# Smaller causal masks and a reordered first part, and a rearranged seam between attention and experts, in a one-core transformer block

## The reference, cut to what matters

```python
x = x + attention(layernorm(x), w_attn, w_proj, embk, embv)   # x: 8 x 512 x 128, 16 heads of 8 dims
x = x + experts(layernorm(x), gate_w, gate_bias, w1, w3, w2, sw1, sw3, sw2)

def attention(x, ...):
    q, k, v = heads(x @ w_attn)
    rel = tril(idx[:, None] - idx[None, :])
    att = q @ k.T / sqrt(8) + einsum('bhtd,tsd->bhts', q, embk[rel])
    att = softmax(where(causal, att, -inf))
    return (att @ v + einsum('bhts,tsd->bhtd', att, embv[rel])) @ w_proj

def experts(x, ...):          # 8 experts, the best 2 by gate, and 2 shared ones, 128 wide
    scores = softmax(x @ gate_w.T); idx = top_k(scores + gate_bias, 2)
    y = sum over e of gate_e * ((silu(x @ w1[e].T) * (x @ w3[e].T)) @ w2[e].T)
    return y + silu(x @ sw1.T) * (x @ sw3.T) @ sw2.T
```

## Time and profile before

| | |
|---|---|
| time, median of 3 runs | 788.38 us (786.87 to 790.86) |
| the profiled execution | 783.03 us |
| its span, first to last instruction | 781.2 us |
| mean granted TensorE clock | 0.977 |
| busy: PE, DVE, ACT, POOL | 699.7, 593.5, 517.5, 255.9 us |
| DMA | 140.32 MB |
| first scores instruction of DVE (L1047) | 59.61 us |
| last exponential of attention (L972) ends | 543.09 us |

### The profile page before, as it was taken

How to read it: one execution, slowest core, us unless ns; L and a number is a source line. 1 busy time by engine, 2 the same in 40 slices (tenths; PEclk the granted TensorE clock), 3 DMA queues, 4 the chain that set the end, 5 groups by cost and what they waited for, 6 DMA issues and landing times. The chain is left out here.

```text
span 781.2 us, 27135 instructions
## 1 busy us (share of the span) xinstructions
PE 699.7 (90%) x10368; PEld 506.4 (65%) x10368; DVE 593.5 (76%) x2036; ACT 517.5 (66%) x1032; POOL 255.9 (33%) x253
## 2 busy tenths in 40 slices
PE   4567879999888899987999988997999999999997
PEld 3345557777666677765777766776666666666665
DVE  8856668888687788877888788887467776776676
ACT  3476877788797778896888898887425334443331
POOL 9343345444346433544633445633000000000000
PEclk9897979999999999999999999999999999999999
DMA  9998998889899878678778769951000000000000
GB/s 303 294 235 293 331 286 264 274 222 286 286 262 290 274 223 261 224 237 244 228 204 268 225 201 274 280 171 49 3 22 28 28 0 28 28 15 1 13 15 14
DMA packets 116687, 140.32 MB, mean 180 GB/s; under 512 B 8848, under 2 KB 83088, under 8 KB 116368
## 3 DMA queue, kind: packets, MB, share of 16 engines
q1 hardware_dynamic: 116560, 138.59, 58.0%
HBM read 82.26 MB, written 56.30 MB: 177 GB/s over the span
## 5 line engine op out<-in xcount | busy, mean ns | idle before, releaser
L1047 DVE CUSTOM_DVE_ANT_0 ps<-ps,near 128x128 f32<-128x128 f32 (+3 forms) x512 | 245.2, 511 | 90.7 <-PE ps L818 57.7
L972 ACT ACTIVATE work<-ps,nmin 128x128 f32<-128x128 f32 (+3 forms) x512 | 249.9, 542 | 65.1 <-DVE nmin L1047 58.4
L830 PE MATMUL ps<-ident,work 128*128 128x128 f32 x1280 | 203.4, 278 | 12.0 <-issue 8.7
L830 PEld LDWEIGHTS ps<-ident,work 128*128 128x128 f32 x1280 | 157.5, 143 | 35.5 <-issue 14.4
L818 PE MATMUL ps<-kb,qb 128*128 128x128 bf16 (+3 forms) x512 | 131.6, 310 | 15.2 <-ACT work L972 11.1
L776 POOL TENSOR_SCALAR_AFFINE_SELECT work<-work 128x512 f32<-128x512 f32 x96 | 61.5, 641 | 238.8 <-ACT work L961 203.5
L1364 ACT ACTIVATE near<-ps 128x512 f32<-128x512 f32 x80 | 47.7, 596 | 134.7 <-PE ps L1329 134.6
L780 POOL TENSOR_TENSOR work<-work 128x512 f32<-128x512 f32 x96 | 124.2, 1293 | 8.0
L1032 DVE COPY work<-ps 128x512 f32<-128x512 f32 (+1 forms) x192 | 123.4, 643 | 3.1 <-PE ps L830 1.5
L1339 PEld LDWEIGHTS ps<-work,near 128*128 128x128 f32 x640 | 82.6, 191 | 34.3 <-issue 31.7
L961 ACT ACTIVATE work<-ps 128x512 f32<-128x512 f32 (+1 forms) x160 | 90.3, 564 | 13.8 <-PE ps L830 13.2
(11 more groups left out here) (110 smaller groups left out, 629.1 us busy)
## 6 DMA issues: line engine op xcount, KB each, us to landing
near<-w_slots SPq DMA_DIRECT2D x96, 512.0 KB, 5.4
w_slots<-relS SPq DMA_DIRECT2D x128, 256.0 KB, 4.7
qk_rows<-work SPq DMA_DIRECT2D x36, 256.0 KB, 5.1
near<-w_slots SPq DMA_DIRECT2D x32, 256.0 KB, 4.9
w_slots<-near SPq DMA_DIRECT2D x8, 512.0 KB, 6.1
qk_rows<-y SPq DMA_DIRECT2D x9, 256.0 KB, 3.3
qb<-qk_rows SPq DMA_DIRECT2D x24, 96.0 KB
kb<-qk_rows SPq DMA_DIRECT2D x24, 96.0 KB
```

What stands on the lines that cost most here:

```text
L830: ins = nc.tensor.transpose(tp_ps[:, m % 2, n * P:(n + 1) * P], prob[:, m % PROBS, n * P:(n + 1) * P], ident[:, :])
L972: ins = nc.scalar.activation(prob[:, m % PROBS, h * wide:(h + 1) * wide], qk_ps[:, m % 3, h * wide:(h + 1) * wide], ACT.Exp, bias=nmin[:, ...
L1047: nc.vector.tensor_tensor_reduce(out=scores, in0=scores, in1=near[:, q % NEAR, a, 4 * P - wide:4 * P, r], scale=1.0, scalar=3e38, op0=ALU. ...
```

## The change

**Masks.** A slot's mask is written in four rectangles instead of whole (`MASKED`): rows 0 to 63 and 64 to 127 apart, without the 64 columns of each that a later `put_rel` fills. One DMA writes a rectangle of one half of the heads into four slots (the source read four times). Slots 0 to 3 are written where all eight were; slots 4 to 7 after `load_first`. Only slots 0 to 3 are waited for ahead of `put_rel`. The source moves from `near[:, 0]` to `near[:, 4]`.

**First part.** Two pairs of `rest` buffers by the parity of g, so `split(g)` waits for POOL's work of g - 2; the table instructions move behind `stats(2)`, the value table into `split(2)`; ACT turns its order at g = 0 (the q rest before the turned copy of group 1); `load_first` is cut in two, and its second K half of batch 1 goes behind the first three `get_near`; PE begins scores after group 3's q is read, and waits for the rest in slot 1.

**Slots.** All relative products of quads with 384 or 512 keys come 14 slots ahead (10 before in the first row), `soon` pieces begin in slot 19 (14 before).

**Seam.** `roots` moves to slot 328 and `inverse` to slot 330 on their engines, `normalise` to slot 352 (353 before). The gate scores and the waits for the last bank readers go behind the first two expert products. The product with `tv` takes another bank, and waits for the gate's reader no more; `yt` does.

```diff
-        ahead = 8 if row(q) <= 1 else 10 if q < QUADS else 14
+        ahead = 8 if row(q) <= 1 else 14
-        at.append(max(reload, FIRST[q] - ahead, *at[-1:]))
+        at.append(max(reload, FIRST[q] - ahead, 1 if q >= MISC else 0, *at[-1:]))
...
-    bank.update({("rv", e): highest, ("yt", e, 0): lowest, ("yt", e, 1): highest, ("yb", e): lowest, ("pj", e): highest})
+    bank.update({("rv", e): highest - 1, ("yt", e, 0): lowest, ("yt", e, 1): highest, ("yb", e): lowest, ("pj", e): highest})
...
-    at.update({14 + 2 * k: [piece] for k, piece in enumerate(soon)})
+    at.update({19 + 2 * k: [piece] for k, piece in enumerate(soon)})
...
+MASKED = ((slice(0, P // 2), 0, P // 2), (slice(0, P // 2), P, 2 * P),
+          (slice(P // 2, P), 0, P), (slice(P // 2, P), P + P // 2, 2 * P))
...
     def masks(sp, lot):
-        for n in lot:
-            sp.dma_start(w_slots[n].rearrange("p a c h -> p a (c h)"),
-                         t["near"][:, 0, :, 2 * P:4 * P, :].rearrange("p a c h -> p a (c h)")
-                         ).then_inc(mask_out, 16)
+        for rows, lo, hi in MASKED:
+            for a in range(2):
+                mask = t["near"][rows, NEAR - 1, a, 2 * P + lo:2 * P + hi, :].rearrange("p c h -> p (c h)")
+                sp.dma_start(w_slots[lot, rows, a, lo:hi, :].rearrange("n p c h -> p n (c h)"),
+                             mask.unsqueeze(1).broadcast_to([P // 2, lot.stop - lot.start, 2 * (hi - lo)])
+                             ).then_inc(mask_out, 16)
...
+    def tensor_begin(pe):
+
+        wait(pe, rest_done, 2 * G - 1)
+        wait(pe, vg_done, G - 1)
...
-            if g + 1 < G:
+            if 0 < g < G - 1:
                 copy_turned(g + 1)
...
+                if (g, n) == (0, 0):
+                    copy_turned(1)
...
         def split(g):
-            wait(dve, p3_done, 2 * g)
+            wait(dve, p3_done, 2 * (g - 1))
...
-            if g == 0:
-                split_tables()
+            if g == G - 2:
+                value_table()
...
-        tables()
         for g in range(G):
             split(g)
             if g + 2 < G:
                 stats(g + 2)
+            if g == 0:
+                tables()
...
-                first["masks"](sp, range(WSLOTS))
+                first["masks"](sp, slice(0, WSLOTS // 2))
...
-                load_first(0)
-                first["values"](sp, 1)
-                first["row"](sp, 1, 1, NPART - 1)
-                sp.wait_ge(*first["masks_out"](WSLOTS))
+                load_first(0, 0)
+                load_first(0, 1)
+                first["masks"](sp, slice(WSLOTS // 2, WSLOTS))
+                sp.wait_ge(*first["masks_out"](1))
                 now = REL_AT.count(0)
                 for q in range(now):
                     put_rel(q)
-                load_first(1)
+                first["values"](sp, 1)
+                load_first(1, 0)
+                first["row"](sp, 1, 1, NPART - 1)
                 for q in range(now):
                     get_near(q)
+                load_first(1, 1)
+                sp.wait_ge(*first["masks_out"](2))
...
-                first["ready"](pe)
-                pe.wait_ge(first["wp_in"], 16)
+                first["begin"](pe)
                 qk(0)
                 for m in range(SLOTS):
+                    if m == 1:
+                        first["ready"](pe)
...
-                for kind, *what in LAST:
-                    pe.wait_ge(*READ[kind](*what))
-                experts["scores"](pe, 0)
...
                         if step == 0:
-                            experts["wait_scores"](pe, 0)
+                            for kind, *what in LAST:
+                                pe.wait_ge(*READ[kind](*what))
+                            experts["scores"](pe, 0)
...
+                            pe.wait_ge(rvn_done, GI)
+                        else:
+                            experts["wait_scores"](pe, 0)
                         yt(e, step - 2)
...
+                    if m == FIRST[NQ - QUADS] + 8:
+                        experts["roots"](act, 0)
                     if m == NU:
-                        experts["roots"](act, 0)
-                    if m == NU + 1:
                         experts["normalise"](act, 0)
...
-                    if m == NU:
+                    if m == FIRST[NQ - QUADS] + 10:
                         experts["inverse"](dve, 0)
```

More of the change, by code:

```diff
@@ L347, in pool_program @@
                 wait(pool, p2_done, 2 * g + 1 + n)
-                nc.gpsimd.tensor_tensor(part(g, n, 2), rest[:, n, :], part(g, n, 1), ALU.subtract).then_inc(p3_done, 1)
+                nc.gpsimd.tensor_tensor(part(g, n, 2), rest[g % 2][n], part(g, n, 1), ALU.subtract).then_inc(p3_done, 1)
     def value_banks(g):
@@ L435, in split @@
                 act.wait_ge(rest_done, 2 * g + 1 + n)
-                nc.scalar.activation(part(g, n, 1), rest[:, n, :], ACT.Copy).then_inc(p2_done, 1)
+                nc.scalar.activation(part(g, n, 1), rest[g % 2][n], ACT.Copy).then_inc(p2_done, 1)
+                if (g, n) == (0, 0):
+                    copy_turned(1)
         stats(0)
@@ L495, in tables @@
             dve.wait_ge(tab, 1)
+            nc.vector.tensor_copy(ekp[:, 0, :], ekr[:, 0, :]).then_inc(tab, 1)
+            dve.wait_ge(tab, 2)
+            nc.vector.tensor_tensor(ekr[:, 1, :], ekr[:, 0, :], ekp[:, 0, :], ALU.subtract).then_inc(tab, 1)
+            dve.wait_ge(tab, 3)
+            nc.vector.tensor_copy(ekp[:, 1, :], ekr[:, 1, :]).then_inc(tab, 1)
+            dve.wait_ge(tab, 4)
+            nc.vector.tensor_tensor(ekp[:, 2, :], ekr[:, 1, :], ekp[:, 1, :], ALU.subtract).then_inc(tab, 1)
@@ L528, in qkv_part @@
             "values_out": lambda g: (v_out[g], 16), "turned": (xnT_done, 2 * (G - 1)),
-            "masks": masks, "masks_out": lambda n: (mask_out, 16 * n), "cleared": ((mask_done, 4), (kb_done, 1)), "tables": (tab, 9), "wp_in": wp_in,
-            "pool": pool_program, "tensor": tensor_program, "ready": tensor_ready, "scalar": scalar_program,
+            "masks": masks, "masks_out": lambda n: (mask_out, 16 * n * 2 * len(MASKED)), "cleared": ((mask_done, 4), (kb_done, 1)), "key_table": (tab, 8), "tables": (tab, 9), "thirds": (p3_done, 2 * (G - 1)), "wp_in": wp_in,
+            "pool": pool_program, "tensor": tensor_program, "begin": tensor_begin, "ready": tensor_ready, "scalar": scalar_program,
             "vector": vector_program}
@@ L890, in first_products @@
                 def first_products(pe):
-                    pe.wait_ge(*first["tables"])
+                    pe.wait_ge(*first["key_table"])
                     for kind, q in OPS[0]:
@@ L900, in _ @@
                 first["tensor"](pe, first_products, first_copied)
-                first["ready"](pe)
-                pe.wait_ge(first["wp_in"], 16)
+                first["begin"](pe)
                 qk(0)
                 for m in range(SLOTS):
+                    if m == 1:
+                        first["ready"](pe)
+                        pe.wait_ge(*first["tables"])
+                        pe.wait_ge(first["wp_in"], 16)
                     if 0 <= m - 3 < NU:
@@ L958, in pT_copy @@
                     act.wait_ge(tp_ready, m + 1)
+                    if m < 2:
+                        act.wait_ge(*first["thirds"])
                     wait(act, av_done, q - 1)
@@ L1029, in pT_copy @@
                     dve.wait_ge(tp_ready, m + 1)
+                    if m < 2:
+                        dve.wait_ge(*first["thirds"])
                     wait(dve, av_done, q - 1)
```

65 lines of the change are left out of this document (28 added, 37 removed).

## The result

The change takes 781.43 us (median of 8 runs, 775.52 to 787.59), beside 789.51 us for the kernel before in the same session. The ratio is 0.9857 (95% interval 0.9825 to 0.9889), 11.3 us less; the two medians lie 8.1 us apart. The ratios in this document are taken over executions in the chip's faster state; the profiled executions of two variants (whole masks, 904.2 us, and the masks alone, 797.62 us) were in the slower one. The forecast was 778.7 us, from 772 to 785, so sign and range hold. The profiled execution took 775.52 us with a span of 773.8, against 783.03 and 781.2: 7.5 us less. Runs of one kernel differ by that much, so ratios come from the timed runs, and a profile is used for single stages.

What follows compares the result with a forecast made beforehand. PE was taken as the bound where full, with transfers and a chain of small steps bounding the beginning. Beginning 5.8 plus seam 3.9 (4.7 less 0.8) gave 9.7 us off the median 788.38: 778.7 us, range 772 to 785.

Steps and rivals of the forecast that it cites:

- rival 1: Beginning: the queue keeps what the chain gives, so it gains only 1 to 3 us; total 782.5 us, chance 0.20.
- My 5.8: Gain in us taken for the beginning, nearer to the queue's 4 than to the chain's 8.
- the queue's 4 us: Beginning's lower bound: loads 4.9 us earlier, less 4.3 for a lot of masks, plus 3.5 of idle DMA time.
- the data after about 8 us: First near load: get_near at 43.5 us, its data about 8 us later, at 51.5, instead of 59.61.
- my own window term: DMA from 32 to 44 us: the second lot of masks brings 4.3 us into a stretch with 3.1 us free.
- below 12 us: DVE's waits for near up to 130 us, 17.5 us in all before, were to fall below 12 us.
- The cost I named as the stall: First part on DVE: L494 (3.52 us), L496 and L498 stood ahead of the q rest; split(0) first saves 3.65 us.
- some 1.9 us: First part on DVE: time saved by moving the six table instructions out of split(0).
- Rival 2: The root costs PE more than the seam gives back; beginning 5.8, seam 1.8, total 780.8 us, chance 0.10.
- Rival 4: Slower: PE in the first 130 us falls to half clock for longer; total 792.9 us, chance 0.04.
- Rival 5: First near still comes near 59 us, SP held issuing masks; only the seam is left, 784.5 us, chance 0.05.
- Rival 3: More than forecast: the chain's 8 us in full and half clock stretches gone, 3 more; 773.5 us, chance 0.11.

Runs made afterwards that it cites:

- whole masks: The change with each slot's mask one 512 KB DMA again and all eight ahead of the first rows: 782.03 us, ratio 0.9847 to the kernel before.
- the masks alone: The kernel before with only the change's masks, in rectangles and two lots: 790.58 us, ratio 0.9978 to the kernel before.
- Parts alone: Beginning: the change with the old seam, 791.53 us, ratio 0.9958. Seam: the kernel before with the change's seam, 790.11 us, ratio 0.9942.
- the second profile of the change: The unaltered change executed again, beside three variants on one chip: 782.11 us, ratio 0.9841 to the kernel before.
- the seam alone: The kernel before with roots, inverse, normalise and expert products as in the change: 790.11 us, ratio 0.9942 to the kernel before.
- `soon` at slot 14: The change with the stores of values 2 and 3 and group 2's Q rows from slot 14, not 19: 777.21 us, ratio 0.98 to the kernel before.
- ten slots of lead: The change with relative products of quads 3 to 7 coming 10 slots ahead, not 14: 787.41 us, ratio 1.0007 to the kernel before.

## Why the prediction was right, and where it was off

**Sign and size.** The sum was 9.7 us. By the ratio it is 11.3 us (8.8 to 13.8), by the medians 8.1, by the profiled executions 7.5. Parts alone give 3.3 (beginning) and 4.6 (seam), 7.9 together, with intervals of 2.5 us each, so no gap between parts and whole is clear of the noise. Stage by stage the terms were each a little too good: 4.9 us at unit 40 for 5.8, 1.25 us of PE for 0.8, 4.1 us at the seam for 4.7, in all 7.7 for 9.7. That the ratio comes out above the sum is no merit of the terms. Part of it may lie in the old seam, which I priced from its shortest execution: 17.59 us, where two other profiles of it have 20.58 and 20.69, all behind the same 3.36 us of idle time. The new seam, with 0.96 us of idle time, was at full clock in every profile but the one of 904.2 us.

**Masks and queue.** Predicted: `load_first` at 27.3 us, two lots of 4.3 us of DMA, half the idle time of 7.1 us staying, so 4 us by the queue. Measured: 27.86 us and 3.4 us idle. Unit 40 starts 3.7 us earlier in the first pair of profiles. Over all profiles of an old beginning (113.03, 114.60, 115.14) and a new one (109.32, 107.99, 111.32, 108.87) it is 114.3 against 109.4, 4.9 us, and the two groups do not overlap. My 5.8 lay between the bounds, and above what came: rival 1's mechanism has more weight than I gave it, the beginning lies nearer to the queue's 4 us.

**The chain.** The copy L950 was forecast for 37.9 us and came at 36.52; `put_rel` 39, and 37.77; `get_near` 43.5, and 44.30; the first scores 51.5, and 53.73. The step that failed is "the data after about 8 us": it took 9.4, and `put_rel` to `get_near` took 6.5 where I had 4.5. I had let the stores and loads pass at an unloaded pace while my own window term had filled the DMA engines by then. The second failed step is the waits for `near` "below 12 us": 15.4 and 15.1, in 7 and in 10 waits for the 12 before, with a longest one of 4.5 and 4.3 us for 3.3. Why they hardly shrank was not separated; SP issues each `get_near` in its order, behind whatever stands in front.

**The cost I named as the stall.** The first place in DVE's order was right: L483 starts at 16.14 us (20.40 before), and the table work behind `stats(2)` delays nobody. 3.65 us were taken for the reorder; 3.2 of it was the 3.52 us of one instruction that takes 0.28 elsewhere. The "some 1.9 us" of the six other table instructions was mis-sized: they ran from 21.54 to 25.45 us, 3.9 us, of which 1.95 was L510's stretch. So `stats(2)` ended its normalising at 26.35 us (24.16 + 2.19), 6.3 us earlier and not 5.5, and the copy L950 came before its forecast.

**The last row.** ACT's extra time was forecast as 2.9 us, and is 510.79 - 507.86 = 2.93. PE's share was forecast as 0.8 and is 1.25, the same in every profile but the one of 904.2 us (units 328 to 333 take 7.47 or 7.48 us in the four kernels without the roots there, 8.72 to 8.74 in the others): mis-sized by 0.45 us, as PE has no slack there and only part of ACT's is used. The Trainium skill (ScalarE: Activation LUTs, What ACT_TABLE_LOAD costs) adds a drain of 1.38 us to every switch of the table. By it the prediction estimated that PE would lose 3.6 us. The trace does not bear that out: the exponential ends at 507.84, the load starts at 507.86, the root 0.02 us behind the load, and PE loses 1.25.

**The seam.** Forecast 12.9 us from the copy to L1339, measured 13.52, 12.96 in the second profile of the change and 13.12 with the seam alone. Each station of the forecast is met within 0.4 us up to the end of the second pair of expert products (9.66 us behind the copy, forecast 9.8). The last pair takes 1.82 us (551.34 to 553.16), as forecast. What was mis-sized is the second half of L863 before it: 2.04 us (549.30 to 551.34) for 1.3, with a wait of 0.63 us in the middle of it. That wait is 0.23 us with the seam alone and absent in the second profile of the change; what PE waits for there is open. The gain of 4.7 was 4.1, less 1.25: 2.8 net in the first pair, 3.4 in the second profile, for 3.9.

**Rivals.** Rival 2 (the root costs more than the seam gives) falls by the stages: 1.25 us lost, 3.6 won, though the timed 2.3 us alone would not decide it. Rival 4 (longer at half clock) falls: unit 40 is earlier and the waits do not rise. Rival 5 falls with `load_first` at 27.86. Rival 3's 8 us of the chain did not come (5.9 at the first scores, 4.9 at unit 40), nor did its half-clock part: the granted clock rose in one window and fell in the next (60 to 66 us from 0.50 to 1.00, 66 to 80 us down to 0.76).

**What stays open.** Why the middle of attention differs by 8.5 us between executions of one kernel; whether `soon` at slot 14 is better; and how 1.9 us at unit 40 become 5 or more in the timed runs with ten slots of lead. The reordered first part (DVE, POOL and ACT) was never run by itself, nor was the split `load_first`, so what the beginning gains is not divided between them and the lead. None of the variants beats the change by more than the intervals.

## What to carry to other kernels

When a transfer is late in a full in-order DMA queue, its position is worth less than it looks, and what stands in front of it may be holding an engine through a buffer: list who waits for each piece before calling it ballast. Take the smaller of what the chain and the queue let through, and price latencies behind a full queue from a loaded stretch. Put what must wait into the stretch where the transfers are idle, as the second lot of masks here, and move a function-table switch from a serial seam into a row that hides part of it (2.93 us on ACT cost 1.25 us there and freed 3.6). Before taking a stage's length as what a change can save, look at the same stage in several executions: the old seam took 17.59 us in one, 20.58 and 20.69 in two others.

## What the hardware showed that I had not expected

- An instruction of DVE took 3.52 us at 15.58 us and 0.28 us at 26.27 us, the same shape and operands. It ended 0.08 us behind a MEMSET of POOL in each of four profiles, wherever it had started; another one, 2.30 us for 0.35, ended 0.14 us behind a TENSOR_TENSOR of POOL. That points to POOL; a run with POOL's work moved was not made.
- A serial seam pays twice. After 3.36 us without work PE ran ten us at 1.2 GHz, where four transposes took 1.09 us instead of 0.63; the old seam cost 17.59 or 20.58 us by how long that lasted (3.4 or 10.2 us), behind the same idle time. With the roots moved the idle time was 0.96 us, and the clock stayed at its upper level (2.4 GHz).
- Eight DMA issues from SP took 7.34, 8.71 or 12.72 us for the same volume of masks, with the DMA engines full each time (shares of 1.01, 0.97 and 1.02): behind a full queue issue time is no fixed price of the instruction. What sets it apart was not separated.
